# Experts' first layer with swapped operands, its weights kept in SBUF, one gelu for a group and the output turned back by transposes

## The chip, the cores and the metric

The kernel runs on one core of a Trainium2 chip. The metric is the device time in microseconds (us). The kernel before was run three times: 1236.9, 1242.91 and 1248.6 us, with a median of 1242.91 us. A further, profiled execution took 1238.02 us, of which the profile shows a span of 1236.2 us from the first to the last instruction.

## The reference

Four blocks follow one another on 8 sequences (one kernel call treats them as 32 tiles of 128 tokens, 128 features wide, fp32): an attention block, a gated feed-forward block, a linear attention block with a three-level MLP, and a mixture of experts that is iterated. The change touches the last one alone:

```python
probs = softmax(gelu(xf @ router_w1 + router_b1) @ router_w2 + router_b2)
topk_p, topk_i = top_k(probs, 2)                    # of 8 experts
for _ in range(2):                                  # ITERS
    ctx = concatenate([integrated, v], -1)          # 128 + 128 features
    for e in range(8):
        h = gelu(ctx @ w1[e] + b1[e])               # 256 -> 64, the first layer
        o = h @ w2[e] + b2[e]                       # 64 -> 384 (a, b, g)
        ctrl = where(idx == e, o, ctrl)
    v_next = sigmoid(a) * v - softplus(b) * (x - mu)
    x_next = x + 0.1 * sigmoid(g) * v_next          # then mixed with the shared expert
```

In the first of the two iterations v is zero, so only the first 128 rows of w1 and two of the three parts of w2 are needed.

## The kernel before

**Tiling.** The tokens are taken in two halves (h = 0, 1) of four sequences. GpSimd scatters the rows of a half, twice each (top 2), into slots in DRAM that are sorted by expert (`scatter`, line 540); every slot tile of 128 rows belongs to one expert. A half has 40 slot tiles, in 10 groups of 4. After the experts the rows are gathered back (`gather`, line 550) and added by VectorE (`update`, lines 964 and 967).

**Order of the work.** `PHASES` (half, iteration) is (0,1), (1,1), (0,2), (1,2). Each phase is a list of 14 groups in `GROUPS`: 4 shared ones ("S", one sequence each) and 10 expert ones ("E"). All engines walk the same list of 56 groups with one step `s` for each, software-pipelined by a fixed order written out by hand. In step s TensorE does `g_control(s)` (second layer, lines 1587 and 1598), `g_hidden(s+2)` (first layer, lines 1616, 1619, 1620) between the two units of the control, and `g_turn(s+3)` (transposes of the input, line 1266). A group of experts in the first iteration has one control unit, all others two.

ScalarE in step s does, in every second step, `soft` (Exp and Ln over two groups with two table loads, lines 1180 to 1185), then `gates(s)` (Tanh, line 1193), `hidden_gelu(s+2)` (lines 1205, 1209) and `turned(s+3)` (copies of the transposed input out of PSUM, lines 1220 and 1222). VectorE copies the b part out of PSUM (line 894), then does the elementwise chain of group s-2, which ends in line 941, and from steps 17, 31 and 45 on the updates of the phase before.

**First layer before.** It is computed in transposed form: the 64 columns of an expert's w1 are the stationary operand (128x64), the transposed inputs `xTs` are the moving one (128 columns). The result is 64 hidden units by 512 tokens in one PSUM bank (2 or 3), which is what the second layer needs as its stationary operand. Since the bias of an expert is one number for each partition, the gelu takes it as its `bias`, in one activation for each of the four tiles, for the tiles belong to different experts.

**The weights before.** SyncE's queue has, for each expert group, `load_w1(s+5)`: it waits until the group four earlier has had its gelu, loads four registers from the table `te` (line 367), and issues four DMAs of 128 rows from DRAM (line 391), one for each tile. Behind it in the same queue come `load_in(s+5)` (the slots, line 381) and `store(s-2)` (the results, line 398). The second layer's weights `EW2` lie in SBUF for all experts; TensorE picks columns with registers that it loads itself from `te2` (line 1567).

## Time and profile before

| what | value |
|---|---|
| three runs | 1236.9, 1242.91, 1248.6 us |
| profiled execution | 1238.02 us, its span 1236.2 us |
| mean granted TensorE clock | 0.865 of 2.4 GHz |
| TensorE matmul, weight load | 852.1 us (69%), 584.9 us (47%) |
| VectorE, ScalarE, GpSimd | 669.6, 565.8, 495.4 us |
| DMA packets | 71481, of them under 512 B 18688 |

An engine's time is the union of its instructions' spans; matmuls are pipelined, so the busy time of TensorE is not its time at peak, and PE stands for matmuls, PEld for weight loads. An fp32 matmul of the program shows as two matmuls and two weight loads in the profile, a transpose as one of each. "x8" behind a row is the number of such records. A bracket at a row's end is the idle time of the engine ahead of it and what ended it; "remote" and "issue" are releasers that the profile could not find.

### The profile page before, as it was taken

What the parts mean: (1) busy time and instruction counts of PE and PEld (TensorE: products, weight loads), DVE (VectorE), ACT (ScalarE), POOL (GpSimd) and SP (SyncE); (2) the same over time, 40 slices, a digit from 0 to 9 for tenths busy, and PEclk for the clock granted to TensorE, in tenths of its full rate; (3) what the DMA queues carried; (4) which work ended last, traced back from release to release, by engine and by line L of the source; (5) the groups of instructions that cost most, each with busy time, mean ns of one, the idle gap of its engine ahead of it and who ended that gap; (6) DMA issues with size and microseconds to landing.
All of it is one profiled execution on the core that took longest, in us unless ns stands there. A gap on an engine that the chain in (4) does not pass through costs nothing.

```text
span 1236.2 us, 13999 instructions
## 1 busy us (share of the span) xinstructions
PE 852.1 (69%) x3906; PEld 584.9 (47%) x3906; DVE 669.6 (54%) x1536; ACT 565.8 (46%) x1036; POOL 495.4 (40%) x436
## 2 busy tenths in 40 slices
PE   3799897657878869888886123767358675868635
PEld 1466665443444436676664112545235452546323
DVE  6412212553575766645657204878355865777733
ACT  2733333534222136565641023876357654767602
POOL 3411101424343562421218776007562665334071
PEclk9999999778998879999987565887679988989887
DMA  9800000000000000000010122355446553634122
GB/s 357 361 1 1 1 0 0 1 0 1 0 1 0 1 0 1 1 1 0 0 52 16 51 73 73 121 164 158 135 166 204 152 155 103 190 101 124 51 68 64
DMA packets 71481, 91.10 MB, mean 74 GB/s; under 512 B 18688, under 2 KB 57600, under 8 KB 69376
## 3 DMA queue, kind: packets, MB, share of 16 engines
q1 hardware_dynamic: 61040, 64.79, 16.4%
q0 software_dynamic: 10240, 25.18, 6.5%
q10 hardware_dynamic: 144, 0.46, 0.2%
q8 instruction: 25, 0.41, 0.1%
q14 instruction: 32, 0.26, 0.1%
HBM read 44.26 MB, written 46.14 MB: 73 GB/s over the span
## 4 chain that ended last, share of the span: by engine, by line
PE 34%; issue 19%; DVE 16%; ACT 16%; another core or an unknown queue 9%; POOL 4%; DMA 1%; ACTq 0%; POOLq 0%; DVEq 0%
PE PS L1422 3%; PE PS L1307 2%; PE PS L1355 2%; PE PS L1315 2%; PE PS L1447 2%; PE PS L1496 2%; PE PS L1344 2%; PE PS L1513 2%; ACT KEEP L1153 2%; PE PS L1616 2%; PE PS L1598 2%; ACT KEEP L1205 2%; PE PS L1260 2%; ACT L1180 1%
## 5 line engine op out<-in xcount | busy, mean ns | idle before, releaser
L550 POOL DMA_INDIRECT KEEP<-moved,small x128 | 127.5, 996 | 210.2 <-DMA moved<-LX 91.8
L540 POOL DMA_INDIRECT slots<-KEEP,small x128 | 132.3, 1033 | 56.7 <-issue 36.6
L1616 PE MATMUL PS<-KEEP,TEMP 128*64 128x128 f32 x480 | 76.5, 321 | 98.2 <-ACT KEEP L1220 56.0
L894 DVE COPY TEMP<-PS 128x256 f32<-128x256 f32 (+1 forms) x92 | 43.2, 477 | 180.8 <-remote 62.4
L1598 PE MATMUL PS<-TEMP,KEEP 128*128 x320 | 110.5, 485 | 17.0 <-ACT TEMP L1193 15.2
L1616 PEld LDWEIGHTS PS<-KEEP,TEMP 128*64 128x64 f32 x480 | 65.0, 164 | 119.0 <-ACT KEEP L1220 63.5
L1193 ACT ACTIVATE TEMP<-PS 128x512 f32<-128x512 f32 (+2 forms) x92 | 51.3, 560 | 105.8 <-DVE TEMP L894 74.0
L482 POOL TENSOR_TENSOR KEEP<-KEEP 128x1024 f32<-128x1024 f32 x32 | 61.7, 1948 | 63.1 <-PE PS L1447 60.3
L1598 PEld LDWEIGHTS PS<-TEMP,KEEP 128*128 128x128 f32 x320 | 64.9, 218 | 43.1 <-issue 27.3
L1496 PE MATMUL PS<-TEMP_R 128*128 128x512 f32 x288 | 75.5, 410 | 12.2 <-POOL TEMP_R L509 8.2
L769 DVE TENSOR_TENSOR TEMP_R<-KEEP,TEMP_R 128x512 fp32r<-128x512 f32 x64 | 62.4, 999 | 34.0 <-ACT KEEP L1153 33.6
L1153 ACT ACTIVATE KEEP<-PS,TEMP 128x512 f32<-128x512 f32 x96 | 69.2, 722 | 15.9 <-PE PS L1496 15.6
L1266 PE MATMUL PS<-WL,TEMP 128*128 128x128 f32 x272 | 45.1, 307 | 40.9 <-DMA TEMP<-slots 34.4
L1260 PE MATMUL PS<-TEMP,KEEP 128*128 128x128 f32 x160 | 28.4, 314 | 60.1 <-POOL KEEP L420 39.2
L1496 PEld LDWEIGHTS PS<-TEMP_R 128*128 128x128 f32 x288 | 53.6, 194 | 32.7 <-issue 10.2
L1205 ACT ACTIVATE KEEP<-PS,TEMP 64x128 f32<-64x128 f32 x160 | 44.5, 355 | 39.1 <-remote 34.8
L1447 PE MATMUL PS<-KEEP,TEMP 128*128 128x512 f32 x128 | 59.9, 605 | 3.5 <-POOL KEEP L482 3.5
L1266 PEld LDWEIGHTS PS<-WL,TEMP 128*128 128x128 f32 x272 | 35.5, 158 | 54.8 <-issue 49.0
L1587 PE MATMUL PS<-WL,KEEP 128*128 128x257 f32 (+1 forms) x128 | 47.9, 509 | 17.4 <-ACT TEMP L1193 11.9
L1220 ACT ACTIVATE KEEP<-PS,WL 128x512 f32<-128x512 f32 x48 | 32.9, 685 | 54.9 <-remote 28.0
L1152 ACT ACTIVATE TEMP_R<-PS,TEMP 128x512 fp32r<-128x512 f32 x64 | 47.0, 734 | 24.0 <-PE PS L1496 24.0
L1508 PE MATMUL PS<-TEMP_R 128*128 128x512 f32 x192 | 49.6, 402 | 9.0 <-ACT KEEP L1153 7.4
(221 smaller groups left out, 1915.8 us busy)
## 6 DMA issues: line engine op xcount, KB each, us to landing
slots<-LX SPq DMA_DIRECT2D x14, 1024.0 KB, 25.1
moved<-LX SPq DMA_DIRECT2D x20, 512.0 KB
TEMP<-slots SPq DMA_DIRECT2D x20, 512.0 KB
TEMP<-experts SPq DMA_DIRECT2D x80, 64.5 KB
TEMP<-slots SPq DMA_DIRECT2D x20, 256.0 KB
moved<-LX SPq DMA_DIRECT2D x20, 256.0 KB
TEMP<-early SPq DMA_DIRECT2D x1, 2829.0 KB, 12.2
TEMP<-experts SPq DMA_DIRECT2D x80, 32.5 KB
```

The costliest lines, as they stand in the source:

```text
L482: pool.tensor_tensor(o, kk, vv, ALU.mult).then_inc(S["c1_kv"], 1)
L540: pool.indirect_dma_start(dst, bass.IndirectOffsetOnAxis(ap=pos[:, h, 2 * m + k:2 * m + k + 1], axis=0), src, None).then_inc(SC[h], 16)
L550: pool.indirect_dma_start(G[:, n % 4, k, 0:w], None, src, bass.IndirectOffsetOnAxis(ap=pos[:, h, 2 * m + k:2 * m + k + 1], axis=0))\
L769: dve.tensor_tensor(Gr[:, k, 1, SEQ * c:SEQ * (c + 1)], d_G[:, k, SEQ * c:SEQ * (c + 1)], Gr[:, k, 0, SEQ * c:SEQ * (c + 1)].bitcast(F32), ...
L1153: act.activation(d_G[:, k, SEQ * c:SEQ * (c + 1)], PS[:, 2 + c, :], ACT.Gelu_apprx_tanh, bias=bias)\
L1205: last = act.activation(hT[0:EHID, e % 3, P * j:P * (j + 1)], PS[0:EHID, bank, P * j:P * (j + 1)], ACT.Gelu, bias=W1[0:EHID, e % 4, j, 0:1])
L1260: last = pe.transpose(PS[:, bank, P * j:P * (j + 1)], src[:, k, j], eye)
L1266: last = pe.transpose(PS[:, bank, P * j:P * (j + 1)], src[:, j], eye)
L1447: last = pe.matmul(PS[:, 4 + 2 * (c % 2) + h, :], we("tril"), kv[:, c % 2, SEQ * h:SEQ * (h + 1)], start=True, stop=True)
L1496: last = pe.matmul(PS[:, 2 + c, :], CWr[:, pw, at:at + P], hTr[:, k, px], start=n == 0, stop=n == 2)
L1598: last = pe.matmul(o, hT[:, e % 3, P * j:P * (j + 1)], EW2[:, bass.ds(at[j], n)], start=True, stop=True)
L1616: last = pe.matmul(PS[0:EHID, bank, part], W1[:, e % 4, j, 1 + EHID * a:1 + EHID * (a + 1)], xTs[:, x % 2, a, part], start=a == 0, stop=a ...
```

## The change

- **Weights.** One DMA at the start of the experts' block loads all experts' first layers and biases (`EW1`, 8 x 192 columns) into SBUF, ahead of the one for `EW2`. `load_w1` is gone, with its 160 DMAs, register loads and waits. TensorE loads the registers from `te` itself and picks columns of `EW1`.
- **Operands.** `g_hidden` has the transposed inputs as the stationary operand (128x128) and 64 columns of `EW1` as the moving one. The result is 128 tokens by 64 units for each tile, 256 columns for a group, in one half of bank 2. The bias is added by one more matmul in each tile: the stationary operand `top` is a 128x128 matrix with ones in its first row, the moving one holds the bias in its first row.
- **Gelu.** One activation over 128x256 for a group, without bias, into `HG` in SBUF.
- **Turning back.** `g_hidden_turn(s+1)`: four transposes of 128x64 to 64x128 into bank 3, between `g_control(s, 0)` and `g_hidden(s+2)`. ScalarE's `hidden_turned(s+1)` copies 64x512 from there into `hT`, between `gates(s, 0)` and `hidden_gelu(s+2)`. The control of a group now waits for this copy (`a_h`), not for the gelu.
- **Banks.** The shared expert's first layer uses bank 3 alone; before it alternated between 2 and 3.

```diff
+            sp.dma_start(EW1, firsts).then_inc(S["w_experts"], 16)
+            sp.dma_start(EW2, seconds).then_inc(S["w_experts"], 16)
...
-            def load_w1(g):
-                _, h, it, i = GROUPS[g]
-                e = EXP_AT[g]
-                sp.wait_ge(S["so_v"], SORT_N * h + 11)
-                if e >= 4:
-                    sp.wait_ge(S["a_g"], HID_AT[EXP_G[e - 4]] + 1)
-                for j, r in enumerate(experts_of(h, i)):
-                    n = 1 + it * EHID
-                    sp.dma_start(W1[:, e % 4, j, 0:n], experts[bass.ds(r, P), 0:n]).then_inc(WA[e % 4], 16)
...
                 if is_e(s + 5):
-                    load_w1(s + 5)
                     load_in(s + 5)
...
                 if kind == "E":
-                    if e >= 3:
-                        act.wait_ge(S["p_q"], UNIT_AT[EXP_G[e - 3] + 1])
-                    for j in range(TILES):
-                        last = act.activation(hT[0:EHID, e % 3, P * j:P * (j + 1)], PS[0:EHID, bank, P * j:P * (j + 1)],
-                                              ACT.Gelu, bias=W1[0:EHID, e % 4, j, 0:1])
+                    need(act, S["p_r"], e - 1)
+                    last = act.activation(HG[:, e % 2].rearrange("p j d -> p (j d)"), PS[:, 2, 256 * (e % 2):256 * (e % 2) + 256], ACT.Gelu)
...
+            def hidden_turned(g):
+                e = EXP_AT[g]
+                act.wait_ge(S["p_r"], e + 1)
+                if e >= 3:
+                    act.wait_ge(S["p_q"], UNIT_AT[EXP_G[e - 3] + 1])
+                act.activation(hT[0:EHID, e % 3], PS[0:EHID, 3, :], ACT.Copy).then_inc(S["a_h"], 1)
...
                 if s < NG:
                     gates(s, 0)
+                if s + 1 < NG and GROUPS[s + 1][0] == "E":
+                    hidden_turned(s + 1)
                 if s + 2 < NG and turned_in(s + 2):
                     hidden_gelu(s + 2)
...
                 else:
-                    pe.wait_ge(S["a_g"], HID_AT[g] + 1)
+                    pe.wait_ge(S["a_h"], e + 1)
...
                 if kind == "E":
-                    pe.wait_ge(WA[e % 4], 64 * (e // 4 + 1))
+                    if e == 0:
+                        pe.wait_ge(S["w_experts"], 32)
+                    if i == 0:
+                        pe.wait_ge(S["so_v"], SORT_N * h + 11)
+                    if e >= 2:
+                        pe.wait_ge(S["a_g"], HID_AT[EXP_G[e - 2]] + 1)
+                    at = columns_of(te, h, i, FIRST_E)
                     for j in range(TILES):
-                        part = slice(P * j, P * (j + 1))
+                        o = PS[:, 2, 256 * (e % 2) + EHID * j:256 * (e % 2) + EHID * (j + 1)]
+                        pe.matmul(o, wl("top"), EW1[:, bass.ds(at[j] + 2 * EHID, EHID)], start=True, stop=False)
                         for a in range(it):
-                            last = pe.matmul(PS[0:EHID, bank, part], W1[:, e % 4, j, 1 + EHID * a:1 + EHID * (a + 1)],
-                                             xTs[:, x % 2, a, part], start=a == 0, stop=a == it - 1)
+                            last = pe.matmul(o, xTs[:, x % 2, a, P * j:P * (j + 1)], EW1[:, bass.ds(at[j] + EHID * a, EHID)],
+                                             start=False, stop=a == it - 1)
                 else:
-                    pe.matmul(PS[0:96, bank, :], wl("gA")[:, 0:96], xTs[:, x % 2, 0], start=True, stop=False)
-                    last = pe.matmul(PS[0:96, bank, :], wl("g1v"), xTs[:, x % 2, 1], start=False, stop=True)
+                    need(pe, S["a_h"], e)
+                    need(pe, S["a_g"], x)
+                    pe.matmul(PS[0:96, 3, :], wl("gA")[:, 0:96], xTs[:, x % 2, 0], start=True, stop=False)
+                    last = pe.matmul(PS[0:96, 3, :], wl("g1v"), xTs[:, x % 2, 1], start=False, stop=True)
                 last.then_inc(S["p_h"], 1)
+
+            def g_hidden_turn(g):
+                x, e = HID_AT[g], EXP_AT[g]
+                pe.wait_ge(S["a_g"], x + 1)
+                need(pe, S["a_h"], e)
+                for j in range(TILES):
+                    last = pe.transpose(PS[0:EHID, 3, P * j:P * (j + 1)], HG[:, e % 2, j], eye)
+                last.then_inc(S["p_r"], 1)
...
                 at = g_control(s, 0, None)
+                if s + 1 < NG and GROUPS[s + 1][0] == "E":
+                    g_hidden_turn(s + 1)
                 if s + 2 < NG and turned_in(s + 2):
                     g_hidden(s + 2)
```

## Rows read from the trace of the kernel before

**Rows 1.** The page's busy times and shares of the span.

```profile
PE 852.1 (69%) x3906; PEld 584.9 (47%) x3906; DVE 669.6 (54%) x1536; ACT 565.8 (46%) x1036; POOL 495.4 (40%) x436
```

**Rows 2.** Windows, experts' block: window, us, busy us (instructions) by engine, granted clock, DMA.

```profile
717.00:764.00 47.00, 11.69 (x39) 8.82 (x40) 6.35 (x18) 8.61 (x15) 37.78 (x38) 0.57 0.23 67
780.00:828.00 48.00, 33.99 (x161) 26.14 (x159) 36.31 (x63) 41.15 (x65) 0.00 (x0) 0.89 0.46 149
832.00:946.00 114.00, 69.24 (x278) 50.18 (x279) 66.24 (x140) 61.84 (x101) 65.52 (x63) 0.73 0.51 158
988.00:1070.00 82.00, 58.00 (x257) 37.26 (x258) 52.41 (x97) 49.32 (x80) 42.28 (x41) 0.88 0.45 135
1107.00:1161.00 54.00, 39.12 (x185) 25.96 (x183) 44.81 (x91) 39.66 (x68) 18.39 (x18) 0.91 0.31 86
```

**Rows 3.** Timeline of phase (0,1), two steps: start, us, engine, line.

```profile
789.40 1.28 ACT L1180 ACT_TABLE_LOAD   x1
...
796.38 1.09 PE L1616 MATMUL PS<-KEEP,TEMP 128*64 128x128 f32 x8 [1.67 <-ACT KEEP L1220]
...
797.40 0.65 PE L1266 MATMUL PS<-WL,TEMP 128*128 128x128 f32 x4
797.51 1.12 ACT L1205 ACTIVATE KEEP<-PS,TEMP 64x128 f32<-64x128 f32 x4 [0.69 <-PE PS L1616]
...
797.89 1.89 PE L1598 MATMUL PS<-TEMP,KEEP 128*128 x8
...
799.22 1.28 ACT L1180 ACT_TABLE_LOAD   x1
```

**Rows 4.** Timeline of phase (1,2), about three steps.

```profile
1127.02 1.96 PE L1616 MATMUL PS<-KEEP,TEMP 128*64 128x128 f32 x16 [0.48 <-ACT KEEP L1222]
...
1132.64 1.28 ACT L1180 ACT_TABLE_LOAD   x1
1132.68 1.96 PE L1616 MATMUL PS<-KEEP,TEMP 128*64 128x128 f32 x16
...
1145.14 1.28 ACT L1180 ACT_TABLE_LOAD   x1
```

**Rows 5.** Timeline of SyncE's queue, 714 to 765 us.

```profile
714.72 0.63 SPq L381 DMA_DIRECT2D TEMP<-slots  x1
716.30 11.35 SPq L391 DMA_DIRECT2D TEMP<-experts  x4
728.35 0.71 SPq L381 DMA_DIRECT2D TEMP<-slots  x1
...
763.17 0.53 SPq L381 DMA_DIRECT2D TEMP<-slots  x1
764.28 1.89 SPq L391 DMA_DIRECT2D TEMP<-experts  x4
```

**Rows 6.** Timeline of the other engines in that stretch.

```profile
729.02 1.09 PE L1266 MATMUL PS<-WL,TEMP 128*128 128x128 f32 x4 [5.39 <-DMA TEMP<-slots]
736.80 1.12 ACT L1205 ACTIVATE KEEP<-PS,TEMP 64x128 f32<-64x128 f32 x4 [11.81 <-remote]
748.08 0.42 DVE L894 COPY TEMP<-PS 128x256 f32<-128x256 f32 x1 [26.80 <-issue]
759.98 0.69 ACT L1220 ACTIVATE KEEP<-PS,WL 128x512 f32<-128x512 f32 x1 [11.06 <-remote]
```

**Rows 7.** Groups by line and shape: busy us, mean ns, idle before.

```profile
L1193 ACT ACTIVATE TEMP<-PS 128x258 f32<-128x258 f32 x12 | 4.5, 386 | 19.6 <-issue 11.9 <-DVE TEMP L894 7.6
L1222 ACT ACTIVATE KEEP<-PS 128x512 f32<-128x512 f32 x28 | 16.7, 597 | 9.1 <-remote 9.1
```

**Rows 8.** TensorE with 8 moving columns (router), before the experts.

```profile
644.66 0.95 PE L1540 MATMUL PS<-WL,KEEP 128*128 128x8 f32 x8
```

**Rows 9.** Register loads of TensorE: duration ns min/median/max.

```profile
L1567 PEldq TENSOR_LOAD <-LX x40: 328/332/840, 763.8 to 1150.8; - x40
```

**Rows 10.** DMA issues, first iteration's expert weights, KB each.

```profile
TEMP<-experts SPq DMA_DIRECT2D x80, 32.5 KB
```

More of the change, by code:

```diff
@@ L72 @@
 sc0 sc1 g_in0 g_in1 g_in2 g_in3 y_out0 y_out1
-xs0 xs1 xs2 xs3 wa0 wa1 wa2 wa3 w_second
-p_t p_h p_q a_x a_g a_t a_l v_b v_ab v_c v_el v_up
+xs0 xs1 xs2 xs3 w_experts
+p_t p_h p_r p_q a_x a_g a_h a_t a_l v_b v_ab v_c v_el v_up
 f_t f_x f_1 f_g f_2 e_t e_x d_xb
@@ L150, with build @@
 MOST, LAST = slice(0, NT - 2 * TILES), slice(NT - 2 * TILES, NT)
-def build(nc, x, early, late, experts, seconds, out):
+def build(nc, x, early, late, firsts, seconds, out):
     with ExitStack() as ctx:
@@ L276, in build @@
         XS = tx(8, TILES, 2 * P)
-        W1 = tx(4, TILES, 1 + 2 * EHID)
+        EW1 = tx(EXPERTS * FIRST_E)
+        HG = tx(2, TILES, EHID)
         EW2 = tx(EXPERTS * 384)
@@ L285, in build @@
         xnb = TEMP[:, 0:NSEQ * SEQ].rearrange("p (a j d) -> p a j d", a=NSEQ, j=TILES)
-        tr_ = cut(TEMP, 8192 + 16 * (1 + 2 * EHID) + EXPERTS * 384 + 16 * 257)
+        tr_ = cut(TEMP, 8192 + EXPERTS * FIRST_E + 2 * TILES * EHID + EXPERTS * 384 + 16 * 257)
         triB, onesB = tr_(64).bitcast(BF16), tr_(64).bitcast(BF16)
@@ L315, in build @@
         XSL = [S[f"xs{n}"] for n in range(4)]
-        WA = [S[f"wa{n}"] for n in range(4)]
         def q_bank(g, u):
@@ L361, in _ @@
             sp.wait_ge(S["ln_rs"], 5)
-            sp.dma_start(EW2, seconds).then_inc(S["w_second"], 16)
-            def experts_of(h, i):
-                row = te[0:1, h, TILES * i:TILES * (i + 1)]
-                return nc.values_load_multi_w_load_instructions(row, engines=[mybir.EngineType.SP], min_val=0, max_val=(EXPERTS - 1) * P,
-                                                                skip_runtime_bounds_check_because="clamped to the last expert")[1]
+            sp.dma_start(EW1, firsts).then_inc(S["w_experts"], 16)
+            sp.dma_start(EW2, seconds).then_inc(S["w_experts"], 16)
             def load_in(g):
@@ L1562, in _, with columns_of @@
             r_ranks(1)
-            def seconds_of(h, i):
-                row = te2[0:1, h, TILES * i:TILES * (i + 1)]
-                return nc.values_load_multi_w_load_instructions(row, engines=[mybir.EngineType.PE], min_val=0, max_val=(EXPERTS - 1) * 384,
+            def columns_of(table, h, i, n):
+                row = table[0:1, h, TILES * i:TILES * (i + 1)]
+                return nc.values_load_multi_w_load_instructions(row, engines=[mybir.EngineType.PE], min_val=0, max_val=(EXPERTS - 1) * n,
                                                                 skip_runtime_bounds_check_because="clamped to the last expert")[1]
@@ L1605, in g_hidden @@
                 x, e = HID_AT[g], EXP_AT[g]
-                bank = 2 + x % 2
                 pe.wait_ge(S["a_x"], PART_AT[g + 1])
@@ L1755, in pack_late, with pack_firsts @@
     put("iwrow", everywhere(f["integration_weight"]))
+    put("top", np.ones((1, P), np.float32))
     return a
-def pack_experts(i):
-    a = np.zeros((EXPERTS, P, EXPERT_N), np.float32)
-    f = {n[len("L1_ffn_"):]: v for n, v in i.items() if n.startswith("L1_ffn_")}
-    a[:, 0:EHID, 0] = f["expert_b1"]
-    a[:, :, 1:1 + EHID] = f["expert_w1"][:, :P]
-    a[:, :, 1 + EHID:1 + 2 * EHID] = f["expert_w1"][:, P:]
-    return a.reshape(EXPERTS * P, EXPERT_N)
+def pack_firsts(i):
+    a = np.zeros((P, EXPERTS, 3, EHID), np.float32)
+    f = i["L1_ffn_expert_w1"]
+    a[:, :, 0] = f[:, :P].transpose(1, 0, 2)
+    a[:, :, 1] = f[:, P:].transpose(1, 0, 2)
+    a[0, :, 2] = i["L1_ffn_expert_b1"]
+    return a.reshape(P, EXPERTS * FIRST_E)
 def pack_seconds(i):
@@ L1786 @@
     arrays = {"x": i["L0_attn_x"].reshape(NSEQ * SEQ, P), "early": pack_early(i), "late": pack_late(i),
-              "experts": pack_experts(i), "seconds": pack_seconds(i)}
+              "firsts": pack_firsts(i), "seconds": pack_seconds(i)}
     nc = _bacc.Bacc("TRN2", target_bir_lowering=False, num_devices=1)
```

18 lines of the change are left out of this document (7 added, 11 removed).

## The prediction, written before the result was known

> **What bounds the kernel now.** I read the page's shares first: no engine is full, TensorE with 852.1 us of matmul records is the busiest [rows 1], so waits and chains decide. The change touches only the experts' block, so I cut that into windows at its phases [rows 2]. Four kinds of stretch show. (a) 717 to 764: 47 us in which TensorE works 11.7, VectorE 6.4 and ScalarE 8.6 us, while GpSimd scatters for 37.8 us: the groups crawl. (b) 780 to 828, phase (0,1): ScalarE is busy 41.2 of 48 us and sets the pace. (c) 832 to 946 and 988 to 1070: GpSimd's gathers and scatters take 65.5 of 114 and 42.3 of 82 us, VectorE's updates wait for them in line, and TensorE has a third of its time free. (d) 1107 to 1161: TensorE 39.1, VectorE 44.8, ScalarE 39.7 of 54 us, a loop through three nearly full engines.
>
> The loops are read from the timelines. In phase (0,1) two steps last from one table load to the next, 789.40 to 799.22, 9.8 us [rows 3]; ScalarE waits in them only for the first layer, 0.69 us ahead of its gelus. In phase (1,2) two steps last 12.5 us (1132.64 to 1145.14), and TensorE's first layer waits for ScalarE's copy of the turned input [rows 4].
>
> **TensorE, the price of one group.** An fp32 matmul is two records. Before, a group of the first iteration has 8 of them in line 1616, in 1.09 us; of the second 16, in 1.96 us [rows 3, 4]: the second 8 add 0.87 us, 0.109 each at full clock. After, the bias makes it 16 and 24 records, of 64 moving columns behind a 128-column weight load. No such record is in the trace. From below: half of 0.109, if the moving columns set the pace. From above: the router's matmul, with 128 columns of weights and 8 moving, takes 0.95 us for 8, 0.119 each less the end of the last [rows 8]; with so little to move that can only be the weight load. I take 0.113, near this end, for the load has the same 128 columns. So the first layer costs 16 x 0.113 - 8 x 0.109 = +0.94 us in the first iteration and 24 x 0.113 - 16 x 0.109 = +0.97 us in the second. The four transposes back take 0.65 us as the input's do [rows 3]. Together +1.6 us a group, 64 us for 40 groups if nothing covers it, which is the outer bound.
>
> **Registers.** TensorE now loads `te` too, 0.33 us in the median and 0.84 at most [rows 9]. The load comes after the wait for the turned input, so it can't be taken early: +0.3 to +0.8 us between ScalarE's copy and the first matmul, in each group where that wait binds; I take 0.4. Queued behind it are the transposes of the next input and the next control.
>
> **ScalarE.** Four gelus take 1.12 us a group [rows 3]. One over 128x256 should take what Tanh over 128x258 takes, 0.386, and the copy of 64x512 what the copy over 128x512 takes, 0.597 [rows 7]: 0.98 us. That saves 0.14 us a group and hides nothing. What matters more is where the copy sits: between gates and gelu, where ScalarE waited 0.69 us before.
>
> **Two steps of phase (0,1).** In the step without table loads the path is: copy of the turned input, TensorE's first layer, gelu, transposes of the input, next copy. It grows by 0.94 + 0.4, loses 0.73 by the shorter gelu (1.12 to 0.39), and gains a wait of about 0.3 for the transposes of the input, which the longer gelus used to hide: +0.9 us for two steps. TensorE's own work comes to 2 x (3.4 + 1.6) = 10.0 us (796.38 to the end of the control at 799.78, and the new 1.6) [rows 3], under the 10.7 of the loop, so it does not bind by itself. Five pairs of expert groups: +4.5 us.
>
> **Phases (1,1) and (0,2).** Here the cover is GpSimd [rows 2]. If it holds, the price is nothing, if it is gone +4.5 and +6.5 us. I take +2 and +3.
>
> **Two steps of phase (1,2).** TensorE went from one first layer to the next in 5.66 us, and idles about 0.5 in such a step, as ahead of the first of the two (0.48), so its work is some 5.1 us a step [rows 4], 6.7 after, 13.4 for two. The loop through ScalarE grows by 0.97 + 0.4 in the step without table loads: 12.5 to 13.9. The longer of the two counts, less 0.1 from ScalarE: +1.3 us for two steps, +6.5 us for five.
>
> **SyncE and the DMAs.** 160 DMAs go, the first iteration's 32.5 KB each [rows 10], and their register loads with them; one load of 0.79 MB (8 x 192 columns x 4 B x 128) comes, issued when the block begins, before the slots are even sorted, so its time costs nothing; behind it in the queue stands `EW2`, needed later still. Four such issues take 1.9 us when GpSimd is quiet, but 11.35 us while it scatters, and so the slots of the second expert group are issued at 728 us and those of the fourth at 763, and not by 718 [rows 5]. TensorE stood 5.39 us for one of them [rows 6]. The rest of the crawl is not theirs: ScalarE stands 11.81 and 11.06 us, VectorE 26.80 us, with a releaser that the profile doesn't find, on work TensorE had long done [rows 6]. I take back 4 us of that first wait. The Trainium skill (DMA: Bandwidth & Descriptors, section SWDGE vs HWDGE vs iDMA) says that GpSimd's generator writes its rings in SBUF and can be disturbed there, while DMAs of the hardware generator, such as SyncE's, never touch that path and are immune; by it SyncE would not be slow beside the scatters, and the 4 us would not be there to take. The rows above show 11.35 against 1.89 us, and I go by them.
>
> **Sum.** 4.5 + 2 + 3 + 6.5 - 4 = +12 us on the profiled execution's 1238 us: **1250 us**. That execution is 4.9 us below the median of the three runs, well inside their spread of 11.7 us.
>
> **Rivals.**
>
> *Freed queue (faster).* The stretch of 47 us is slow only once SyncE's many DMAs meet GpSimd's scatters. For it: the slowness starts at 716, with SyncE's first batch, and SyncE's own issues are slow too [rows 5]; with five DMAs less four, all slots would be on their way by 718. Against it: ScalarE and VectorE wait where no DMA of SyncE is due [rows 6]. It decides if ScalarE's first gelu comes right after 725 instead of 736.8. Price: the stretch shrinks by up to 38 us (763 to 725), I take 35; like stalls beside gathers may shrink by some us more. 1238 + 16 - 35 = 1219 us.
>
> *Cheap swap.* The 64-column records take half of 0.109 after all: the first layer then costs 0 and -0.43 us, and what is left are the transposes, 0.65, in TensorE's idle time, and the register load. ScalarE's shorter gelu pays for that. 1238 - 4 + some 3 = 1237 us. The Trainium skill (TensorEngine Tiling (Array Packing), section Instruction Overhead) has a rule this way: a matmul costs about 60 cycles of overhead, so that few columns are as fast as 60; by it alone 64 columns would be nearly free. The router's row, where 8 columns take 0.119 us, speaks against it.
>
> *TensorE binds throughout (slower).* The extra 1.6 us show in every second-iteration group, since register loads stall the queue and the stalls keep the clock low (0.73 granted between 832 and 946 [rows 2]): 20 x 1.6 = 32 us, +4.5 + 2 - 4: 1272 us. It decides if TensorE never idles over 0.3 us in phase (1,2).
>
> **How the numbers follow.** Changes under 1% (1230.5 to 1255.3 us) can't be told from none. My sum holds with 0.5, between 1238 and 1265 us, for the cover of two phases and the register load are each uncertain by some 5 us; 0.3 of that lies below 1255. Freed queue 0.28, cheap swap 0.12 (all within), TensorE throughout 0.1. Faster 0.28, same 0.42, slower 0.30. The likeliest case alone spans 1238 to 1265. The range for 8 in 10 has to take in part of the freed queue and of the slow case: 1215 to 1272 us.
>
> **What would show it.** Line 1616's successor: 16 or 24 records in 1.8 or 2.7 us at full clock (0.9 or 1.3: cheap swap). The period of the table loads: 10.7 us in phase (0,1), 13.8 in phase (1,2). The new transposes 0.65 us, the gelu 0.39, the copy 0.60. The slots of the first four expert groups issued by 720. The first expert gelu after 725: at once, and the freed queue is right; 10 us later, and it is wrong. I am wrong if the phases with gathers change by more than 10 us, for I have given them almost nothing, or if stalls with no releaser come or go elsewhere.

## The result

The changed kernel takes 1293.67 us (median of 4 runs, 1292.19 to 1299.51), the kernel before beside it 1241.95 us (4 runs, 1236.9 to 1248.6): ratio 1.042, 95% interval 1.036 to 1.048. The forecast was 1250 us, in a range from 1215 to 1272: the kernel is 44 us slower than the one and 22 us slower than the upper end of the other. The same pair gave 1.037 (1.028 to 1.047) and 1.033 (1.029 to 1.037) in the second and third set of the experiments below, on two chips. Some executions of a kernel are over 1.5% longer than its fastest one; ratios and stretches leave them out. The profiled execution took 1299.51 us, its span is 1297.7 us, the mean granted clock 0.845 against 0.865.

The page's busy times after, answering to [rows 1]:

```profile
PE 927.5 (71%) x4386; PEld 661.7 (51%) x4386; DVE 671.0 (52%) x1536; ACT 557.5 (43%) x956; POOL 490.4 (38%) x436
```

TensorE is busy 75 us more, ScalarE 8 us less. The windows by stage, moved with the groups, answer to [rows 2] (same columns):

```profile
721.00:768.00 47.00, 10.23 (x39) 8.59 (x40) 1.40 (x3) 6.69 (x9) 37.79 (x39) 0.54 0.22 67
790.00:852.00 62.00, 44.32 (x241) 37.59 (x239) 36.14 (x62) 40.98 (x54) 0.00 (x0) 0.86 0.29 98
857.00:982.00 125.00, 79.05 (x377) 59.92 (x377) 67.39 (x143) 59.50 (x82) 64.27 (x63) 0.77 0.39 127
1035.00:1127.00 92.00, 69.05 (x308) 46.76 (x307) 52.12 (x96) 48.54 (x69) 39.39 (x40) 0.81 0.35 112
1165.00:1221.00 56.00, 43.88 (x254) 32.67 (x253) 44.88 (x91) 38.41 (x57) 17.69 (x18) 0.97 0.25 74
```

The second line is the news. In phase (0,1) GpSimd does nothing, so its DMAs can't be what costs time there; ScalarE and VectorE are as busy as before (41.0 and 36.1 us), TensorE works 10 us more, and the stretch lasts 62 us instead of 48. The timeline of two steps there answers to [rows 3] (start, us, engine and line; the bracket is the idle time before and its releaser):

```profile
804.31 1.28 ACT L1164 ACT_TABLE_LOAD   x1
...
807.76 1.28 ACT L1169 ACT_TABLE_LOAD   x1
...
809.06 0.60 ACT L1177 ACTIVATE TEMP<-PS 128x512 f32<-128x512 f32 x1
...
809.55 0.58 ACT L1197 ACTIVATE KEEP<-PS 64x512 f32<-64x512 f32 x1
...
810.80 2.41 PE L1585 MATMUL PS<-TEMP,KEEP 128*128 x8 [2.90 <-ACT KEEP L1197]
813.00 1.06 PE L1622 MATMUL PS<-WL,TEMP 128*64 128x128 f32 x4
813.25 0.69 DVE L878 COPY TEMP<-PS 128x512 f32<-128x512 f32 x1 [3.33 <-PE PS L1585]
...
813.97 0.60 ACT L1177 ACTIVATE TEMP<-PS 128x512 f32<-128x512 f32 x1 [3.00 <-DVE TEMP L878]
...
816.65 0.38 ACT L1186 ACTIVATE TEMP<-PS 128x256 f32<-128x256 f32 x1 [1.60 <-PE PS L1608]
...
816.89 1.89 PE L1585 MATMUL PS<-TEMP,KEEP 128*128 x8
...
817.79 1.28 ACT L1164 ACT_TABLE_LOAD   x1
```

Read it as a ring. ScalarE goes through the table loads, Exp, Ln and a Tanh (804.31 to 809.6), and only then copies the turned hidden layer back (line 1197). TensorE's control matmuls (line 1585) have stood 2.90 us for that copy; VectorE's copy stands 3.33 us for them, and ScalarE's next Tanh 3.00 us for VectorE. Before, the control of a group (line 1598) waited for a gelu that ScalarE had done two steps ahead, and ran beside the table loads, Exp and Ln. Of the kernel before:

```profile
788.45 2.92 PE L1598 MATMUL PS<-TEMP,KEEP 128*128 x8
...
790.70 1.06 ACT L1182 ACTIVATE LX<-LX 128x1024 f32<-128x1024 f32 x1
...
792.82 1.89 PE L1598 MATMUL PS<-TEMP,KEEP 128*128 x8
792.86 1.28 ACT L1185 ACT_TABLE_LOAD   x1
```

Two steps now last 817.79 - 804.31 = 13.5 us, against 9.8 for the same two [rows 3]. It is one of the pairs that grew most: by the table loads the five pairs of the phase grew by 3.6, 3.7, 1.9, 3.9 and 0.6 us.

Behind that wait the clock of TensorE falls too. The windows around it (granted clock is the third value from the end):

```profile
808.00:811.00 3.00, 0.20 (x1) 0.20 (x2) 1.85 (x3) 2.96 (x5) 0.00 (x0) 1.00 0.08 33
811.00:813.00 2.00, 2.00 (x8) 1.51 (x8) 0.00 (x0) 0.00 (x0) 0.00 (x0) 0.81 0.53 213
813.00:815.00 2.00, 2.00 (x11) 1.89 (x10) 1.72 (x3) 1.03 (x2) 0.00 (x0) 0.50 0.00 0
816.00:818.00 2.00, 2.00 (x16) 1.87 (x16) 0.69 (x1) 1.27 (x3) 0.00 (x0) 1.00 0.28 96
```

TensorE does nearly nothing for 3 us, then works without a gap, and in the middle of that work the clock falls from 2.4 to 1.2 GHz (0.50 from 813 to 815). The eight control records that started at 810.80 take 2.41 us, the next eight, at the full clock again (816.89), 1.89. The Trainium skill (TensorE: Matmul & The Clock Gate, section HAM oscillation — how this bites in real kernels) tells of a kernel in which waits make TensorE start each next piece of work at the lower clock. This trace agrees only in part: slow work follows the wait, but it starts at the full clock (1.00 until 811). Over the whole phase the clock decides little: in two other executions of the changed kernel (f1 and g1 below) the mean granted clock there is 0.81, in this one 0.86, and they take 62.5 and 62.4 us against 61.9.

Where the loss lies over the whole block, from the ends of VectorE's last operation of each group (line 941 before, 925 after), three executions of the changed kernel (the first pair's, f1 and g1 below):

| stretch | before | after, 1st | 2nd | 3rd |
|---|---|---|---|---|
| start to the last shared group of (0,1) | 780.2 | 790.1 | 784.9 | 787.1 |
| expert groups of (0,1) | 46.9 | 61.9 | 62.5 | 62.4 |
| shared, experts of (1,1) | 26.9, 91.5 | 27.4, 102.6 | 36.9, 92.5 | 37.1, 99.8 |
| shared, experts of (0,2) | 32.9, 91.3 | 43.6, 101.5 | 35.7, 102.7 | 33.1, 102.1 |
| shared, experts of (1,2) | 36.5, 61.7 | 37.1, 63.9 | 37.2, 63.7 | 36.7, 63.4 |
| to the end | 68.3 | 69.7 | 69.8 | 69.7 |

The expert groups of (0,1) repeat to 0.6 us: +15. The middle phases together take 25 to 33 us more, and there one execution differs from the next by up to 10 us in a stretch.

The middle phases and the first stretch hold waits with no releaser. The row pairs that answer to [rows 6] and [rows 5] (the other engines, then SyncE's queue):

```profile
766.93 0.38 ACT L1186 ACTIVATE TEMP<-PS 128x256 f32<-128x256 f32 x1 [38.09 <-remote]
766.99 0.42 DVE L878 COPY TEMP<-PS 128x256 f32<-128x256 f32 x1 [40.92 <-remote]
```

```profile
718.37 49.24 SPq L376 DMA_DIRECT2D TEMP<-slots  x6
```

The weights' DMAs are gone and the first five of these six slot loads were issued by 723, the sixth waits for TensorE; yet ScalarE stands 38 us, to 8 us after the last scatter (758.17). The change did free SyncE's queue. It was not what held the groups up: f2 and f4 below, whose weights still come through that queue, have the first expert gelu at 763.9 and 767.2 us, as late as here.

### The profile page after: what moved, and what is told of

The parts are those of the page before. It is cut to its first block, busy times and chain, and to the rows that moved or that the text cites. A ratio compares the mean times of both kernels' runs of the same rounds, so it can differ in the third digit from the quotient of the medians.

```text
span 1297.7 us, 14800 instructions
## 1 busy us (share of the span) xinstructions
PE 927.5 (71%) x4386; PEld 661.7 (51%) x4386; DVE 671.0 (52%) x1536; ACT 557.5 (43%) x956; POOL 490.4 (38%) x436
## 3 DMA queue, kind: packets, MB, share of 16 engines
q1 hardware_dynamic: 38144, 57.69, 12.7%
## 4 chain that ended last, share of the span: by engine, by line
PE 41%; issue 20%; DVE 13%; ACT 11%; another core or an unknown queue 10%; POOL 4%; DMA 1%; ACTq 0%; POOLq 0%; DVEq 0%; SPq 0%
PE PS L1585 5%; PE PS L1608 3%; PE PS L1411 2%; PE PS L1296 2%; PE PS L1344 2%; PE PS L1304 2%; PE PS L1436 2%; ACT KEEP L1137 2%; PE PS L1485 2%; PE PS L1333 2%; PE PS L1502 2%; PE PS L1606 2%; PE PS L1255 2%; PE PS L1249 1%
## 5 line engine op out<-in xcount | busy, mean ns | idle before, releaser
L524 POOL DMA_INDIRECT slots<-KEEP,small x128 | 128.2, 1002 | 71.5 <-issue 36.6
L1585 PE MATMUL PS<-TEMP,KEEP 128*128 x320 | 119.4, 515 | 45.6 <-ACT KEEP L1197 32.9
L1585 PEld LDWEIGHTS PS<-TEMP,KEEP 128*128 128x128 f32 x320 | 67.1, 225 | 73.9 <-issue 59.9
L1608 PE MATMUL PS<-TEMP,KEEP 128*128 x480 | 93.4, 311 | 0.0
L1485 PE MATMUL PS<-TEMP_R 128*128 128x512 f32 x288 | 79.3, 431 | 11.2 <-POOL TEMP_R L493 8.2
L1606 PE MATMUL PS<-TEMP,WL 128*128 x320 | 71.5, 310 | 21.3 <-ACT KEEP L1209 10.5
L466 POOL TENSOR_TENSOR KEEP<-KEEP 128x1024 f32<-128x1024 f32 x32 | 61.7, 1949 | 63.3 <-PE PS L1436 60.4
L1608 PEld LDWEIGHTS PS<-TEMP,KEEP 128*128 128x128 f32 x480 | 80.0, 227 | 0.0
L753 DVE TENSOR_TENSOR TEMP_R<-KEEP,TEMP_R 128x512 fp32r<-128x512 f32 x64 | 61.8, 990 | 35.0 <-ACT KEEP L1137 34.9
L1485 PEld LDWEIGHTS PS<-TEMP_R 128*128 128x128 f32 x288 | 58.5, 208 | 30.5 <-issue 10.2
L1606 PEld LDWEIGHTS PS<-TEMP,WL 128*128 128x128 f32 x320 | 58.0, 226 | 28.8 <-issue 28.5
L1622 PE MATMUL PS<-WL,TEMP 128*64 128x128 f32 x160 | 28.9, 312 | 50.9 <-ACT TEMP L1186 39.6
L1576 PE MATMUL PS<-WL,KEEP 128*128 128x257 f32 (+1 forms) x128 | 48.3, 514 | 12.8 <-ACT TEMP L1177 6.3
L1136 ACT ACTIVATE TEMP_R<-PS,TEMP 128x512 fp32r<-128x512 f32 x64 | 46.3, 724 | 24.1 <-PE PS L1485 24.0
```

Of the source, the lines that this page charges most:

```text
L466: pool.tensor_tensor(o, kk, vv, ALU.mult).then_inc(S["c1_kv"], 1)
L524: pool.indirect_dma_start(dst, bass.IndirectOffsetOnAxis(ap=pos[:, h, 2 * m + k:2 * m + k + 1], axis=0), src, None).then_inc(SC[h], 16)
L753: dve.tensor_tensor(Gr[:, k, 1, SEQ * c:SEQ * (c + 1)], d_G[:, k, SEQ * c:SEQ * (c + 1)], Gr[:, k, 0, SEQ * c:SEQ * (c + 1)].bitcast(F32), ...
L1485: last = pe.matmul(PS[:, 2 + c, :], CWr[:, pw, at:at + P], hTr[:, k, px], start=n == 0, stop=n == 2)
L1585: last = pe.matmul(o, hT[:, e % 3, P * j:P * (j + 1)], EW2[:, bass.ds(at[j], n)], start=True, stop=True)
L1606: pe.matmul(o, wl("top"), EW1[:, bass.ds(at[j] + 2 * EHID, EHID)], start=True, stop=False)
```

## The experiments

Eighteen kernels ran in five sets, those of a set on one chip; each ratio is to the kernel before, run beside them. In the first set the kernel before takes 1156.5 us, in the other four 1234.5 to 1248.4. "(0,1)" below is the time of the ten expert groups of phase (0,1), measured as in the table: 46.9 us before, 61.9 to 62.5 after.

**First set: take parts of the turning back away, or move them.**

```
e1   if s + 1 < NG and ...: hidden_turned(s + 1)   # now first in ScalarE's step,
     soft(s // 2 - 1); gates(s, 0)                 # it stood behind these
e2   e1, and TensorE: g_hidden_turn(s + 1); at = g_control(s, 0, None)
e3   no g_hidden_turn, no hidden_turned; control waits for a_g and reads zeros
e4 - pe.matmul(o, wl("top"), EW1[:, bass.ds(at[j] + 2 * EHID, EHID)], ...)
```

> ScalarE alone is reordered: the copy back for group s+1 comes first in step s, ahead of the gates' Exp and Ln and of the gates' Tanh; nothing is added or left out. Theory A (late copy): the time over the kernel before is mostly TensorE waiting in its control matmuls for that copy, which stands behind Exp, Ln and the Tanh: 1270 us (1262 to 1280), the steps of phase (0,1) back to about 5.3 us each from 6.4, and the waits of the control matmuls for the copy gone. Theory B (TensorE's added work): the work stays, 1290 us (1285 to 1298). Theory C (longer stops beside GpSimd's scatters and gathers): 1285 to 1298 as well, with the control matmuls' waits moved to other instructions.

> As the run before it, and TensorE too turns the hidden layer of group s+1 back before the control matmuls of group s instead of behind them, so that the copy back is a whole step ahead of its reader. Theory A: as good as the run before it or some us better, 1265 us (1255 to 1280); worse than it only if TensorE now waits for the gelu that has just been issued. Theories B and C: no change from the changed kernel, 1285 to 1298.

> The changed kernel without the turning back: no transposes and no copy back, the control matmuls wait for the gelu and read a hidden layer that nobody writes (zeros). Its time is that of the swap, of the bias matmuls and of the table load on TensorE alone. Theory A: the turning back is what costs, 1240 us (1225 to 1252). Theory B: half of TensorE's added work goes (4 transposes, 0.65 us a group of 40), 1268 us (1260 to 1275). Theory C: if the stops by the scatters follow from these instructions, near A; if they do not, 1280 to 1295.

> The changed kernel without the bias matmuls of the experts' first layer (4 matmuls a group, 0.22 us each, 35 us of TensorE's time over 40 groups); its bias is left out. Theory A: TensorE has time left over where the loop sets the step, and the bias matmuls stand before the gelu and not between copy and control: 1284 us (1276 to 1292). Theory B: 1262 us (1255 to 1272). Theory C: no change, 1288 to 1297.

Measured: e1 1178.1 us, 1.020 (1.016 to 1.023), (0,1) 61.8 us. e2 1169.4, 1.012 (1.009 to 1.016), 59.1. e3 1160.8, 1.004 (1.001 to 1.006), 48.0. e4 1170.0, 1.010 (1.004 to 1.016), 63.6. The absolute expectations assumed another chip; the changed kernel itself was not in this set, so a ratio here is not compared with 1.042. The lengths of (0,1) can be: e2's 59.1 us came again in the third set (g2), on a chip of the slower kind, though GpSimd still scatters for 21 us of that stretch here and not there. Leaving the turning back out wins 14 of the 15 us; the swap with its bias matmuls and register load costs 1. Leaving the bias matmuls out wins nothing there, against theory B. (The whole of e4 is 8 us under the whole of e1; without the changed kernel on this chip it can't be said what of that the bias matmuls are.) But moving the copy ahead within ScalarE wins nothing either, against theory A as I had it. TensorE's waits in e1's expert groups of (0,1), then all engines' largest (engine, line waited for, total us, times, longest):

```profile
PE PS L1622 <- ACT TEMP L1186: 7.2, 3, 2.4
PE PS L1576 <- ACT TEMP L1177: 5.9, 2, 3.1
PE PS L1606 <- issue: 1.5, 3, 0.6
PE PS L1585 <- ACT KEEP L1197: 1.3, 1, 1.3
```

```profile
ACT KEEP L1197 <- PE PS L1622: 10.3, 4, 3.0
PEld PS L1622 <- ACT TEMP L1186: 8.4, 3, 2.8
DVE TEMP L878 <- PE PS L1585: 7.8, 3, 3.7
```

In the changed kernel the control's wait for the copy was 13.0 us in that stretch; here it is 1.3, but TensorE waits 7.2 us in the transposes for the gelu, which ScalarE does behind Exp and Ln too, and ScalarE itself stands 10.3 us for the transposes before it can start Exp. The wait moved.

On this chip the stop beside the scatters is missing. Of e1:

```profile
728.89 1.28 ACT L1169 ACT_TABLE_LOAD   x1
729.63 0.42 DVE L878 COPY TEMP<-PS 128x256 f32<-128x256 f32 x1 [2.76 <-PE PS L1576]
730.47 0.38 ACT L1186 ACTIVATE TEMP<-PS 128x256 f32<-128x256 f32 x1
```

The first expert gelu comes at 730.47, in the same program part and beside the same scatters where it came at 766.93 above. From 700 us on no wait of TensorE, VectorE or ScalarE over 8 us is without a releaser here. And the phases (1,1) and (0,2) together, shared groups included, take 206.2 us in e4, which has the whole turning back with its wait, and 207.8 in e3, which has none of it (e1 206.7, e2 205.1). On this chip GpSimd's gathers and scatters do cover the turning back in those phases.

**Second set: add TensorE's work without the wait, and take other parts alone.**

```
f1   the changed kernel, unchanged
f2 + pe.transpose(PS[:, bank, ...], XS[:, e % 8, j, 0:P], eye)          # x4
   + pe.matmul(PS[:, bank, ...64 columns], eye, W1[..., 1:1 + EHID])    # x4
f3 - at = columns_of(te, h, i, FIRST_E)
   + at = [FIRST_E * ((TILES * i + j) // 5) for j in range(TILES)]
f4 + pe.matmul(PS[0:EHID, bank, part], W1[..., 0:EHID], wl("top"), ...) # bias row
   - four gelus with bias
   + act.activation(hT[0:EHID, e % 3], PS[0:EHID, bank, :], ACT.Gelu)
```

> The changed kernel unchanged, beside the kernel before, on another day's chip: the first four experiments ran where the kernel before takes 1157 us and TensorE's completion signals came at once. Theory A (late copy back): the ratio there is about that of the first pair less what the late signals added, 1.03 (1.025 to 1.045), so 1190 us where before is 1157. Theory C (half or more of the 52 us were late signals beside the scatters and gathers): 1.02 (1.01 to 1.025), 1178 us, no more than with the copy moved first.

> The kernel before, with TensorE's added work alone and no new wait: ahead of the first layer of each expert group 4 transposes of 128x128 and 4 matmuls of 64 columns, written into the bank that the first layer then overwrites; weights still come through SyncE and the output is the same. It is 1.5 us more TensorE work a group, 60 us in all. Theory B (work): ratio 1.02 to 1.03. Theory A (the wait, not the work): ratio 1.005 (1.0 to 1.012), with the phases of two layers the ones that grow.

> The changed kernel with fixed expert columns in the first layer: TensorE loads no registers from the table there (one table load a group less, about 0.4 us, 40 of them), so wrong experts' weights are used. If the register load stands in the loop as I had it: 8 us less than the changed kernel; if TensorE has that time to spare: 2 us less or none; if its wait for the table hides a fetch that delays the queue behind it: 15 us less or more.

> The kernel before, with one of the change's ideas and without the swap: weights still come through SyncE (with a bias row of 64 columns instead of one column), 4 bias matmuls of 128 columns put the bias into the bank, and one gelu over the group's 512 columns replaces 4. No turning back, no registers on TensorE. ScalarE saves about 0.5 us a group, TensorE works 0.9 us more. If ScalarE's four gelus set the step of phase (0,1): ratio 0.99 (0.98 to 1.0). If TensorE's added work weighs as much: 1.0 (0.995 to 1.008). If 33% more bytes of weights weigh: over 1.01.

Measured: f1 1284.3 us, 1.037 (1.028 to 1.047). f2 1268.8, 1.028 (1.018 to 1.038). f3 1274.7, 1.035 (1.024 to 1.047), by its interval not told apart from f1. But three of f3's four executions (1265.7, 1274.5 and 1275.0 us, the fourth 1290.4) lie under all of f1's (1278.9 to 1287.8), some 10 us by the medians, near the 8 us expected for a register load in the loop. In (0,1) f3 wins nothing (61.7 us); its phases (1,1) and (0,2) take 252.3 us, f1's 267.8, in one execution each. So the register load probably costs time in those phases, and how much is open. f4 1254.7, 1.014 (1.005 to 1.023), the branch over 1.01 of its expectation; 12.7 of the 17.9 us by which its profiled execution is longer lie in the first stretch, and whether the bytes of its weights or its added matmuls do that is not shown.

f2 went against theory A's number: the work alone costs 29 of f1's 45 us. In (0,1) it takes 52.2 us, so the work placed like this costs 5 there and the wait some 10. Most of f2's loss is elsewhere, beside indexed DMAs: the first stretch (787.3 against 780.2 us) and the phases (1,1) and (0,2) (263.1 against 242.6, of it 37.6 against 26.9 in the shared groups of (1,1)). VectorE's waits at its copy, over the span, before, after and f2 (line 894 before and in f2, 878 after):

```profile
L894 DVE COPY TEMP<-PS 128x256 f32<-128x256 f32 (+1 forms) x92 | 43.2, 477 | 180.8 <-remote 62.4 <-PE PS L1587 48.0 <-issue 38.3
```

```profile
L878 DVE COPY TEMP<-PS 128x256 f32<-128x256 f32 (+1 forms) x92 | 43.8, 480 | 231.8 <-remote 116.5 <-PE PS L1585 72.2 <-PE PS L1576 39.6
```

```profile
L894 DVE COPY TEMP<-PS 128x256 f32<-128x256 f32 (+1 forms) x92 | 43.7, 479 | 207.0 <-remote 105.2 <-PE PS L1587 52.6 <-PE PS L1598 27.8
```

A wait put down to "remote" in one execution is put down to "issue" in another (the 26.80 us at 748.08 of [rows 6] are "issue"), so the two go together: 100.7 us before, 100.2 in h3 below, which does the same work; 120.0, 131.3 and 138.8 in three executions of the changed kernel, 126.4 in f2, 123.6 in f4 and 124.1 in i1 below, which all have more TensorE instructions. That is 19 to 38 us more, though why is not shown. f4 keeps 46.3 us in (0,1), with ScalarE busy 36.7 us there instead of 40.1. So ScalarE's work did not set the pace of that phase, as the prediction had it, and one gelu for a group had nothing to win there.

**Third set: take the indexed DMAs away.**

```
g1   the changed kernel        g2   e2
g3, g4 (kernel before, changed kernel):
  - pool.indirect_dma_start(dst, IndirectOffsetOnAxis(ap=pos[...]), src, None)
  + pool.dma_start(dst[P * (2 * m + k):P * (2 * m + k + 1)], src)     # gathers alike
```

> The changed kernel unchanged once more, to have its ratio beside the others of this call; chips differ by 7% in the time of the kernel before (1157 and 1240 us), by the 40 us stop of TensorE's signals beside GpSimd's scatters and the shorter ones beside its gathers. Theory A (late copy, work on the path): 1.03 on either kind of chip. Theory C (more is lost in those stops because TensorE has more to do between them): 1.037 where before takes 1240 us, 1.02 to 1.028 where it takes 1157 us.

> Turn back one step earlier on TensorE and copy back ahead of Exp, Ln and Tanh on ScalarE, beside the changed kernel in the same call. Theory A: 0.98 to 0.985 of the changed kernel's time on either kind of chip (1.012 of before where before takes 1157 us, 1.017 to 1.022 where it takes 1240). Theory C alone: 0.995 to 1.005 of the changed kernel's time where before takes 1240 us.

> The kernel before with plain DMAs on GpSimd's queue in place of its scatters and gathers through indices (the same number, rows and bytes, the rows as they come, so tokens reach the wrong experts' slots). If it is the indirect form that holds TensorE's signals up: the stops with no releaser at 725 to 763 and beside the gathers go, 1175 us (1150 to 1195) where before takes 1240 us, 1150 where it takes 1157. If it is the bytes or the descriptors of any GpSimd DMA: within 10 us of before.

> The same with the changed kernel. Its ratio to the run before it is the change's cost without the stops: Theory A 1.03 (1.02 to 1.035), Theory C 1.00 to 1.015.

Measured: g1 1288.8 us, 1.033 (1.029 to 1.037). g2 1275.7, 1.020 (1.014 to 1.026), (0,1) 59.1 as in e2. g3 1097.5, 0.879 (0.874 to 0.884). g4 1140.6, 0.913 (0.908 to 0.918). With plain DMAs both kernels are 148 to 151 us faster, over twice what I had expected, and no wait of VectorE's copy is put down to an unknown releaser any more. Of g3:

```profile
L892 DVE COPY TEMP<-PS 128x256 f32<-128x256 f32 (+1 forms) x92 | 43.0, 478 | 55.2 <-PE PS L1585 36.2 <-PE PS L1596 18.8
```

So the stops go with the indexed form, on a chip that has them. (A plain scatter also takes GpSimd 0.54 us and an indexed one 1.03, so 150 us is more than the stops alone, and whether the form or the pace matters is not told apart.) The change's cost stays: 1140.6 - 1097.5 = 43 us, a ratio of 1.039, just above theory A's 1.02 to 1.035. Theory C, that half of it were the stops, fell. With less of GpSimd in the way the cost is spread: (0,1) 47.1 to 62.4 us, experts of (1,1) 57.5 to 71.0, of (0,2) 68.6 to 77.5, of (1,2) 60.0 to 63.7. That is 15 and 13.5 us in the first iteration, where two steps are short, 9 and 4 us in the second, where the other work of a step is longer. Of g4 over the whole span:

```profile
L1583 PE MATMUL PS<-TEMP,KEEP 128*128 x320 | 115.0, 501 | 53.3 <-ACT KEEP L1195 39.7 <-ACT TEMP L1175 13.2 <-issue 0.3
```

The control waits 39.7 us for the copy back (line 1195 there). I read most of the 43 us as the ring; no kernel with plain DMAs and the copy elsewhere was run to show it.

**Fourth set: give the ring more slack.** The hidden layer, gelu and input's turn of expert groups one step earlier.

```
h1 - g_hidden(s + 2) ... g_turn(s + 3)      hidden_gelu(s + 2) ... turned(s + 3)
   + g_hidden(s + 3) ... g_turn(s + 4)      hidden_gelu(s + 3) ... turned(s + 4)
h2   h1 and e1       h4   h1 with g4's DMAs
h3   the shift in the kernel before, its shared groups of iteration 2 included
```

> The changed kernel with an expert group's hidden layer, gelu and turn of its input one step earlier on TensorE and ScalarE (three and four steps ahead of its control matmuls instead of two and three); the turn back and the copy back stay where they are. Moving the copy back alone left phase (0,1) at 61.8 us against 62, for TensorE then waited at its transposes for the gelu of ScalarE's step before, behind Exp and Ln; here that gelu is a step older. Theory A2 (the wait for the copy back and the wait for the gelu are one round trip between two queues): the expert groups of phase (0,1) take 54 us (50 to 57) instead of 62, the copy still standing behind Exp and Ln; in all 10 to 20 us less than the changed kernel, ratio 1.02 (1.01 to 1.028). Theory B (TensorE's work alone): 61 us there, ratio 1.03 or more.

> The same, and ScalarE's copy back ahead of Exp, Ln and Tanh. Theory A2: both waits gone, the expert groups of phase (0,1) at 50 us (48 to 53), near the 52.2 us of the kernel before with TensorE's added work and no wait; ratio 1.012 (1.005 to 1.022). Theory B: as the changed kernel, 1.03.

> The kernel before with the same shift, no part of the change: hidden layer and gelus three steps ahead, the input's turn four. Tells what the shift is worth by itself: if the kernel before has no round trip in its loop, 1.0 (0.995 to 1.005) and 46 to 48 us for the expert groups of phase (0,1); if the extra slack helps over the stops too, 0.985 to 0.995.

> The first kernel of this call with plain DMAs on GpSimd's queue in place of scatters and gathers (tokens reach wrong slots). Without indices the kernel before took 1097 us, the changed one 1141. Theory A2: 1120 us (1110 to 1128), so half of the 43 us is the round trip. Theory B: 1136 or more.

Measured: h1 1301.3 us, 1.055 (1.050 to 1.060), (0,1) 63.5. h2 1298.0, 1.047 (1.039 to 1.054); of it the ratio alone is used. h3 1246.5, 1.011 (1.006 to 1.015), 47.8, in the stretch as expected. h4 1153.4 us, where g4 took 1140.6 on another chip. Theory A2 missed in h1, h2 and h4, and what theory B had said came for all three; i1 below speaks against B in (0,1). With the copy in its place the gelu's age doesn't matter (h1); and h2 has an older gelu and the copy ahead of Exp and Ln, and is not fast either. h1's waits of TensorE in (0,1) (its control is line 1591, its copy back 1203):

```profile
PE PS L1591 <- ACT KEEP L1203: 12.8, 5, 3.2
PE PS L1582 <- ACT TEMP L1183: 3.7, 2, 3.2
```

12.8 us for the copy, as in the changed kernel. Why the shift makes the kernels slower rather than leaving them alone is open.

**Fifth set: take the copy back off ScalarE.**

```
i1 - act.activation(hT[0:EHID, e % 3], PS[0:EHID, 3, :], ACT.Copy).then_inc(S["a_h"], 1)
   + dve.tensor_copy(hT[0:EHID, e % 3], PS[0:EHID, 3, :]).then_inc(S["a_h"], 1)
     # in VectorE's step s: copy_b(s, 0); this one; copy_b(s, 1); abs_b(s)
i2   i1 and h1
```

> The changed kernel with the copy back on VectorE, between its two parts of a step's copies, instead of on ScalarE behind Exp, Ln and Tanh; nothing else moves. Moving it within ScalarE left the expert groups of phase (0,1) at 61.8 (62 before that), and a step's shift of the layer at 63.5. Theory A3 (ScalarE's order: whatever TensorE needs from it stands behind 4.7 us of Exp, Ln and table loads every second step, and the copy back adds 0.6 us a group to ScalarE itself): the wait for the copy goes, the wait of the transposes for the gelu stays: 57 us (54 to 60) there, 10 us less than the changed kernel in all, ratio 1.028 (1.018 to 1.036). Theory B (TensorE's work and the clock it loses at each wait): 60 to 63 us, ratio 1.035 to 1.045.

> Copy back on VectorE and the hidden layer, gelu and input's turn a step earlier: neither copy nor gelu of the turning back stands behind Exp and Ln for TensorE any more, and ScalarE has less to do a group than in the kernel before. Theory A3: 51 us (48 to 54) for the expert groups of phase (0,1), near the 52.2 of the kernel before with the added TensorE work; ratio 1.015 (1.0 to 1.025). Theory B: 58 us or more there, 1.035 or more in all.

Measured: i1 1262.6 us, 1.015 (1.006 to 1.024), (0,1) **47.6 us**. i2: 1267, 1268, 1291 and 1293 us, too far apart for a ratio; (0,1) 51.9, inside the 48 to 54 expected, but 4 us more than i1, so the shift costs time here too. In i1 the whole 15 us of that stretch are gone, more than the 5 I had expected, and outside the ranges of both theories. The window of (0,1), and its two steps:

```profile
786.00:833.00 47.00, 38.95 (x235) 32.70 (x234) 38.79 (x67) 34.65 (x45) 0.00 (x0) 0.92 0.38 129
```

```profile
794.83 1.28 ACT L1175 ACT_TABLE_LOAD   x1
...
796.49 0.67 DVE L959 COPY KEEP<-PS 64x512 f32<-64x512 f32 x1
...
798.30 1.89 PE L1587 MATMUL PS<-TEMP,KEEP 128*128 x8
...
804.87 1.28 ACT L1175 ACT_TABLE_LOAD   x1
```

VectorE copies at 796.49, under ScalarE's Exp and Ln, TensorE's control runs at 798.30 without a wait, and two steps take 10.0 us. TensorE does all the work of the change, transposes and bias matmuls and register loads included, and the stretch is as long as before (TensorE is busy 39.0 us at a granted clock of 0.92, where the changed kernel has 44.3 at 0.86 and the kernel before 34.0 at 0.89). So the 15 us come from the copy standing in ScalarE's queue, and not from TensorE's added work. They are not the ten copies' own time either, which is 5.8 us; and another place in the same queue is no cure, as e1 shows. Over the whole kernel i1 is 22 us slower than the kernel before where the changed one is 40 to 52. What is left of i1's loss lies in the stretches with indexed DMAs: 785.7 against 780.2 at the start, 35.4 against 26.9 in the shared groups of (1,1), 103.3 against 91.3 in the experts of (0,2). Of the versions that compute the reference none was faster than the kernel before. With the swap in them, e2 (1.012 on the first set's chip, 1.020 on another) and i1 (1.015) come nearest; without it, h3 and f4 have 1.011 and 1.014.

## Why the prediction was wrong, by its own steps

By the stretches of the table, over three executions, the sum lacked 10.5 to 11 us in (0,1), 20 to 27.5 in the two middle phases and 9 to 14 in the first stretch, where it had taken 4 off; it had 4 too many in (1,2). The middle phases are the largest of these, and only part of them is explained below; the failed step that an experiment settles is that of (0,1).

**Prices: right.** 16 records of the first layer take 1.74 us (819.05 to 820.79), 0.109 each where I had 0.113: with 64 moving columns the weight load sets the pace, and "cheap swap" falls. The transposes take 0.60 us (0.65), the gelu 0.377 (0.386), the copy 0.578 (0.597), the register load 0.333 in the median (0.33).

**Two steps of phase (0,1): the step that failed.** It said 9.8 to 10.7 us, +4.5 in all. Measured 13.5 us and +15. I followed the path through the first layer (input's copy, first layer, gelu, input's transposes) and lengthened it. I said of the copy back that its place matters, "between gates and gelu, where ScalarE waited 0.69 us before", and looked only at what it delays there, not at who waits for it: the control matmuls, which before had a whole step of slack and ran under Exp and Ln. The ring from control through VectorE's copy and the Tanh to the copy back and the next control stands in no sentence of mine. i1 shows it: that one operation elsewhere, 13.5 becomes 10.0 us. Its premise, that ScalarE "sets the pace" there, was wrong as well: with 3.4 us less to do for ScalarE (f4) the phase was 0.6 us shorter.

**TensorE's work lies beside other work in (0,1): right** in that it "does not bind by itself". With the wait gone it costs nothing measurable there (47.6 against 46.9 us), while f2 lost 5 us with the same amount of work, placed ahead of the first layer.

**Phases (1,1) and (0,2): wrong, by the test I had set.** +2 and +3 were forecast; the experts alone took 1 to 11 and 10 to 11 us more, with the shared groups 11 to 19 and 11 to 21. Why is shown only in part. "If it holds, the price is nothing" came true of the turning back on the chip without the stops, where e4 and e3, with and without it, take 206.2 and 207.8 us for the two phases. On chips with the stops the two phases take 242.6 us before, 261.7 in i1 and 263.1 in f2, which have work of the change but not the ring, and 267.8 to 275.1 in the changed kernel. That points to the added work for the larger part and to the ring for the smaller. But f3, with the ring and without the register loads, takes 252.3, and executions of one kernel differ by 7 us in this sum. So the shares stay open, and so does how TensorE's work costs time beside the stops.

**Phase (1,2): too high as a sum.** +6.5 was forecast, +1.7 to +2.2 us came for the expert groups. The pair of [rows 4] grew from 12.5 to 13.5 us by the table loads (1191.91 to 1205.44), near my 13.8, and the pair ahead of it from 13.6 to 14.6; but the one ahead of that only from 15.4 to 15.5, and the one behind went from 12.3 to 12.1. The growth was sized rightly for one pair and did not stand for all five.

**SyncE, -4 us, and "freed queue": wrong.** The queue was freed and the groups crawled on: the stretch grew by 5 to 10 us. My own deciding point was the first expert gelu: 736.8 us before, 766.9 after. SyncE's slow issues [rows 5] and the crawl stand side by side, but the slow issues did not cause the crawl; in g3, beside plain scatters, both are gone (four weight issues take 1.88 to 2.36 us there). The rule of the Trainium skill that I had set against my 4 us (DMA: Bandwidth & Descriptors, section SWDGE vs HWDGE vs iDMA) does not say what I drew from it: SyncE's DMAs are immune, by it, to VectorE's hold on the memory in which GpSimd's generator writes. It says nothing of SyncE beside GpSimd's scatters, and nothing of waits for TensorE's finished work, which is what stopped here.

**"TensorE binds throughout"** had 0.1 and gave 1272 us, nearer than my forecast but for another reason: TensorE in phase (1,2) still waits (once 4.8 us for a Tanh), and the loss was largest where I had not put it. So it is luck in the main that its 1272 us lie nearer; by f3 its register loads may have a share in the middle phases.

## What to carry to other kernels

When an operation moves to an engine that works in order, write down two lists: what it delays behind it, and who waits for it, and from when to when that waiter could run before. A wait that had a step of slack and now ends behind a long block of its engine can cost most of that block, whatever the operation's own time: here the block is 4.7 us of table loads, Exp and Ln, the copy takes 0.58 us, and two steps grew by 3.7. If such a ring appears, try another engine for the small operation before shifting the pipeline: i1 won 15 us in the stretch, while e1, e2 and h1, which rearrange ScalarE and TensorE, won 3 at most.

## What the runs showed of the hardware

- Beside GpSimd's indexed DMAs, engines that wait for TensorE's finished work stood up to 41 us in the first pair (VectorE at 766.99, after 40.92 us), and VectorE 38 to 42 us in every kernel with TensorE's added work that was profiled in four of the five sets, the plain-DMA ones excepted. In the other set no such stop is seen, and the kernel before is 84 us faster (1156.5 against 1240). With plain DMAs from the same queue nothing of the kind was seen. What differs between the chips was not found.
- The clock of TensorE fell from 2.4 to 1.2 GHz not in the idle time of 2.90 us but during the work after it (1.00 to 811, 0.50 from 813 to 815), and eight control records took 2.41 us in place of 1.89.
- Less work for TensorE did not make (0,1) shorter: e4, without the bias matmuls, took 63.6 us there at a mean granted clock of 0.79, where the changed kernel took 61.9 to 62.5 at 0.81 to 0.86. Each is one execution, and the difference is too small to build on.
- TensorE's records with a new stationary operand each follow one another at the same pace for few and many moving columns: at the full clock 16 records with 64 columns take 1.74 us (819.05 to 820.79), 0.109 each; the second 8 of 16 records with 128 columns took 0.87 [rows 3, 4], 0.109 each as well; and with 8 columns it was 0.119 with the last one's end [rows 8].
